# The attention's output projection as fp16 products of high and low halves

## The reference

```
h   = tokeniser(x)                         # three levels, joined, times Wf
n   = layernorm(h)
q, k, v = split(n @ W_qkv);  q = elu(q)+1;  k = elu(k)+1     # 12 heads of 16
kv  = sum over tokens of k^T v;  z = 1 / (q . sum(k) + eps)
att = (q kv) z                             # "the divided rows", 256 x 192 a picture
h   = h + att @ W_out + b_out              # the projection
h   = h + mixture_of_experts(layernorm(h)) # 16 experts, 4 for each token
```

## Time and profile before

| | |
|---|---|
| runs | 592.57, 580.58, 574.64 us; median 580.58 us |
| the profiled execution | 569.85 us, of which the span from the first to the last instruction is 568.0 us |
| PE busy | 422.3 us (74%) |
| DVE busy | 329.8 us (58%) |
| POOL busy | 303.2 us (53%) |
| ACT busy | 249.8 us (44%) |
| mean granted TensorE clock | 0.893 of full speed |
| DMA | 42.64 MB, 75 GB/s on average |

### The profile page before, as it was taken

One profiled execution on the slowest core, in us unless ns is written; L12 is line 12 of the kernel. 1 busy time (PEld: TensorE's weight loads), 2 busy tenths in 40 slices (PEclk: granted clock), 3 DMA queues, 4 the chain that ended last, 5 costly groups with the idle time before them and its releaser, 6 DMA issues.

```text
span 568.0 us, 10275 instructions
## 1 busy us (share of the span) xinstructions
PE 422.3 (74%) x2889; PEld 281.9 (50%) x2889; DVE 329.8 (58%) x836; ACT 249.8 (44%) x570; POOL 303.2 (53%) x362
## 2 busy tenths in 40 slices
PE   0017548488999953399789999999999998899940
PEld 0016115445565642255356666666666666666630
DVE  0567876736465452987346557566666566657530
ACT  1677442244444421111155556555555555556520
POOL 7888810003234422000148888778888887778750
PEclk9999999889789885555589999999999999999995
DMA  8886644600000000001114444444443443443436
GB/s 234 226 232 173 182 129 118 184 2 1 19 25 14 15 15 29 9 28 43 42 47 60 65 67 61 66 67 61 66 66 59 66 68 59 68 66 59 66 37 111
DMA packets 36430, 42.64 MB, mean 75 GB/s; under 512 B 8731, under 2 KB 27693, under 8 KB 36381
## 3 DMA queue, kind: packets, MB, share of 16 engines
q0 software_dynamic: 16976, 18.94, 21.6%
q1 hardware_dynamic: 17694, 22.25, 13.8%
q10 hardware_dynamic: 1710, 0.80, 0.6%
HBM read 27.48 MB, written 14.49 MB: 74 GB/s over the span
## 4 chain that ended last, share of the span: by engine, by line
PE 27%; issue 24%; POOL 18%; DVE 14%; DMA 9%; ACT 4%; SPq 2%; ACTq 0%; DVEq 0%; POOLq 0%
POOL R L358 10%; POOL out L367 3%; DMA R<-t_dram,Li 3%; PE pair L1099 3%; PE pair L1098 2%; DMA R<-in_m 2%; DMA out<-R,Li 2%; POOL acc_odd L367 2%; DVE W1s L396 1%; PE pair L1032 1%; DVE W1s L394 1%; PE pair L934 1%; PE pair L935 1%; PE pair L1033 1%; DVE W2s L398 1%
## 5 line engine op out<-in xcount | busy, mean ns | idle before, releaser
L693 DVE TENSOR_SCALAR R<-pair 128x384 f32<-128x384 f32 x79 | 44.1, 558 | 91.5 <-PE pair L1141 56.4
L358 POOL DMA_INDIRECT R<-t_dram,Li x79 | 81.8, 1035 | 24.3 <-issue 23.1
L367 POOL DMA_INDIRECT out<-R,Li x40 | 64.0, 1600 | 21.3 <-issue 10.6
L1159 PE MATMUL pair<-W2s,R 128*128 x711 | 71.7, 246 | 0.8 <-ACT R L861 0.8
L367 POOL DMA_INDIRECT acc_odd<-R,Li x39 | 63.0, 1616 | 14.3 <-issue 10.4
L849 ACT ACTIVATE R<-pair 128x384 f32<-128x384 f32 x79 | 38.8, 492 | 72.1 <-PE pair L1141 42.2
L297 POOL DMA_INDIRECT R<-in_x,idx_sb x42 | 56.7, 1351 | 13.3 <-issue 12.5
L1159 PEld LDWEIGHTS pair<-W2s,R 128*128 128x128 f16 x711 | 60.5, 98 | 2.6 <-issue 1.0
L1137 PE MATMUL pair<-W1s,R 128*128 x158 | 52.3, 331 | 0.0
L1141 PE MATMUL pair<-W1s,R 67*128 x158 | 52.0, 329 | 0.0
L1139 PE MATMUL pair<-W1s,R 128*128 x158 | 51.7, 327 | 0.0
(11 more groups left out here) (229 smaller groups left out, 826.5 us busy)
## 6 DMA issues: line engine op xcount, KB each, us to landing
h_all<-in_m1a SPq DMA_DIRECT2D x11, 384.0 KB
WQK<-in_m SPq DMA_DIRECT2D x11, 288.0 KB
h_all<-in_m1c SPq DMA_DIRECT2D x11, 192.0 KB
WA<-in_m1a SPq DMA_DIRECT2D x5, 384.0 KB
acc_odd<-lz SPq DMA_DIRECT2D x17, 96.0 KB, 2.0
W1s<-W1s SPq DMA_DIRECT2D x1, 1536.0 KB, 10.4
t_dram<-R SPq DMA_DIRECT2D x8, 192.0 KB, 2.0
out<-h_all SPq DMA_DIRECT2D x8, 192.0 KB, 2.0
```

The costliest lines, as they stand in the source:

```text
L358: po.indirect_dma_start(out=Gr32[:, t % RING, :], out_offset=None, in_=t_dram, in_offset=bass.IndirectOffsetOnAxis(ap=Li[:, t:t + 1], axis ...
L367: po.indirect_dma_start(out=(out, acc_odd)[t % 2], out_offset=bass.IndirectOffsetOnAxis(ap=Li[:, t:t + 1], axis=0), in_=yv[:, t % 4, :], i ...
L693: ve.tensor_scalar(lin[:, p, :], bank[2 + 2 * p][:, 0:HID], (LIMIT + 1) * S1, (1 - LIMIT) * S1, ALU.min, ALU.max).then_inc(s_lin, 1)
L1159: ins = mm(bank[5][:, 0:D], a[:, p, P * m:P * (m + 1)], W2s[:, e, w, D * m:D * (m + 1)], start=k == 0, stop=k == 3 * HC - 1)
```

## The change

The divided rows `att` are split as the other operands are: ACT casts them to fp16 (`high_att`, queued after `copy_tpT` and before `kv_parts`), DVE subtracts for the low half (`low_att`, two instructions, queued between `phi_k` and `phi_q`), and PE transposes the resulting 128 x 384 fp16 rows in three pieces a tile, 6 transposes a picture, where it did 4 in fp32. PE's `att_transposes` waits for `low_att` and no longer for `divide`. `copy_attT` becomes one activation of 128 x 768 fp16 elements. `attT` has one buffer where it had two. `project` is 7 fp16 matmuls a tile: two over a single row (ones times the bias's high and low half) and the five of the pattern above. The result carries the factor 512, which `second_statistics` takes out with a scalar_tensor_tensor in place of the tensor_tensor. Before the loop, ACT and DVE make the halves of the output weights and of the bias, with three more instructions each, in the place of the raw q/k/v weights, which are no longer needed there; SP loads the last 64 rows of the weights twice, and the bias by a DMA of its own that waits for the q/k/v weights to be split. POOL's memset of the ones is gone. The diff, with lines of context left out:

```diff
@@ -78,6 +78,9 @@
         GS = sb("GS", [P, 2, NE])
+        WO16 = WA[:, 0:2 * D].bitcast(F16).rearrange("p (k n) -> p k n", k=4)
+        WOB = WA[0:1, 2 * D:3 * D]
+        WOB16 = WA[0:1, 3 * D:4 * D].bitcast(F16).rearrange("p (k n) -> p k n", k=2)
         GS16 = sb("GS16", [P, 4, NE], F16)
@@ -154,7 +157,8 @@
         att, zz = carve([2, D]), carve([2, 2 * NH])
-        attT = carve([2, 2, 256])
+        attT = carve([3, 256], F16)
+        ar = carve([2, 2 * D], F16)
         tp = carve([2, 2, D])
@@ -188,6 +192,7 @@
+        attb = bank[6][:, 0:384].bitcast(F16)
@@ -208,7 +213,7 @@
         s_phk = sem("s_phi_k"); s_phq = sem("s_phi_q")
-        s_stt = sem("s_state"); s_kvm = sem("s_state_masked"); s_nd = sem("s_num_den"); s_atr = sem("s_att_rows"); s_att_t = sem("s_att_transposed")
+        s_stt = sem("s_state"); s_kvm = sem("s_state_masked"); s_nd = sem("s_num_den"); s_atr = sem("s_att_rows"); s_ath = sem("s_att_high"); s_atl = sem("s_att_low"); s_woh = sem("s_out_weights_high"); s_wol = sem("s_out_weights_low"); s_wob = sem("s_out_bias_loaded"); s_att_t = sem("s_att_transposed")
         s_att = sem("s_attT_copied"); s_o = sem("s_attention_out"); s_h2 = sem("s_h2")
@@ -263,11 +268,14 @@
             sp.dma_start(WO[:, 0, :], wo[0:P, :]).then_inc(s_aw, 16)
-            sp.dma_start(WO[0:D1 + 1, 1, :], wo[P:D + 1, :]).then_inc(s_aw, 16)
+            sp.dma_start(WO[0:D1, 1, :], wo[P:D, :]).then_inc(s_aw, 16)
+            sp.dma_start(WO[D1:P, 1, :], wo[P:D, :]).then_inc(s_aw, 16)
             sp.dma_start(B2[:, :], b2).then_inc(s_aw, 16)
...
+            sp.wait_ge(s_al, 1)
+            sp.dma_start(WOB, wo[D:D + 1, :]).then_inc(s_wob, 16)
             sp.wait_ge(s_z, 1)
@@ -308,8 +316,6 @@
             po.memset(vx[:, :, :, :], 1.0).then_inc(s_ms, 1)
-            po.wait_ge(s_ms, 2)
-            po.memset(attT[D1:D1 + 1, :, 1, :], 1.0).then_inc(s_ms, 1)
@@ -346,7 +352,7 @@
-            po.wait_ge(s_ms, 4)
+            po.wait_ge(s_ms, 3)
@@ -457,7 +463,7 @@
-            ve.wait_ge(s_aw, 16 * 6)
+            ve.wait_ge(s_aw, 16 * 7)
@@ -536,16 +542,22 @@
                 link(ve, ve.reciprocal(z, z))
-                wait(ve, s_att_t, b)
+                wait(ve, s_ath, b)
                 ve.tensor_tensor(att.rearrange("p t (h d) -> p (t h) d", d=HD), nd[:, :, 0:HD],
...
+            def low_att(b):
+                ve.wait_ge(s_ath, b + 1)
+                ve.tensor_tensor(ar[:, :, D:D + D1], att[:, :, P:D], ar[:, :, P:D], ALU.subtract)
+                ve.tensor_tensor(ar[:, :, D + D1:2 * D], att[:, :, 0:P], ar[:, :, 0:P], ALU.subtract).then_inc(s_atl, 1)
+
             def second_statistics(b):
...
                 ve.wait_ge(s_o, b + 1)
-                link(ve, ve.tensor_tensor(h2, h2, bank[6][:, 0:2 * D].rearrange("p (t n) -> p t n", t=2), ALU.add))
+                link(ve, ve.scalar_tensor_tensor(out=h2, in0=bank[6][:, 0:2 * D].rearrange("p (t n) -> p t n", t=2),
+                                                 scalar=1.0 / SQ, in1=h2, op0=ALU.mult, op1=ALU.add))
                 for j in range(2):
@@ -585,6 +597,14 @@
             low_normal(1)
+            ve.wait_ge(s_woh, 1)
+            ve.scalar_tensor_tensor(out=WO16[:, 1, :], in0=WO[:, 0, :], scalar=SQ, in1=WO16[:, 0, :],
+                                    op0=ALU.mult, op1=ALU.subtract)
+            ve.scalar_tensor_tensor(out=WO16[0:D1, 3, :], in0=WO[0:D1, 1, :], scalar=SQ, in1=WO16[0:D1, 2, :],
+                                    op0=ALU.mult, op1=ALU.subtract)
+            ve.scalar_tensor_tensor(out=WOB16[:, 1, :], in0=WOB, scalar=SQ, in1=WOB16[:, 0, :],
+                                    op0=ALU.mult, op1=ALU.subtract).then_inc(s_wol, 1)
+
             phi_k(0)
@@ -600,6 +620,9 @@
                     phi_k(s + 1)
+                if s < NB:
+                    low_att(s)
+                if s + 1 < NB:
                     phi_q(s + 1)
@@ -742,7 +765,7 @@
-            ac.wait_ge(s_aw, 16 * 6)
+            ac.wait_ge(s_aw, 16 * 7)
@@ -752,7 +775,12 @@
                               ACT.Copy).then_inc(s_he, 1)
-            ac.wait_ge(s_ms, 3)
+            ac.wait_ge(s_al, 1)
+            ac.activation(WO16[:, 0, :], WO[:, 0, :], ACT.Copy, scale=SQ)
+            ac.activation(WO16[:, 2, :], WO[:, 1, :], ACT.Copy, scale=SQ)
+            ac.wait_ge(s_wob, 16)
+            ac.activation(WOB16[:, 0, :], WOB, ACT.Copy, scale=SQ).then_inc(s_woh, 1)
+            ac.wait_ge(s_ms, 2)
@@ -785,11 +813,14 @@
             def copy_attT(b):
-                p = b % 2
                 ac.wait_ge(s_att_t, b + 1)
-                wait(ac, s_o, b - 1)
-                ac.activation(attT[:, p, 0, :], bank[6][:, 0:256], ACT.Copy)
-                ac.activation(attT[0:D1, p, 1, :], bank[6][0:D1, 256:512], ACT.Copy).then_inc(s_att, 1)
+                wait(ac, s_o, b)
+                ac.activation(attT.rearrange("p c n -> p (c n)"), attb, ACT.Copy).then_inc(s_att, 1)
+
+            def high_att(b):
+                ac.wait_ge(s_atr, b + 1)
+                wait(ac, s_att_t, b)
+                ac.activation(ar[:, :, 0:D], att, ACT.Copy).then_inc(s_ath, 1)
@@ -818,6 +849,8 @@
                     copy_tpT(s - 2)
+                if s < NB:
+                    high_att(s)
                 if s + 1 < NB:
@@ -835,7 +868,7 @@
-            ac.wait_ge(s_ms, 4)
+            ac.wait_ge(s_ms, 3)
             def copy_tile(t):
@@ -936,10 +969,10 @@
-            pe.wait_ge(s_aw, 16 * 6)
+            pe.wait_ge(s_aw, 16 * 7)
-            pe.wait_ge(s_ms, 3)
+            pe.wait_ge(s_ms, 2)
@@ -1015,22 +1048,28 @@
             def att_transposes(b):
-                p = b % 2
-                pe.wait_ge(s_atr, b + 1)
+                pe.wait_ge(s_atl, b + 1)
                 wait(pe, s_h2, b)
                 for j in range(2):
-                    pe.transpose(bank[6][:, P * j:P * (j + 1)], att[:, j, 0:P], ident)
-                    ins = pe.transpose(bank[6][0:D1, 256 + P * j:256 + P * (j + 1)], att[:, j, P:D], ident)
+                    for c in range(3):
+                        ins = pe.transpose(attb[:, 256 * c + P * j:256 * c + P * (j + 1)],
+                                           ar[:, j, P * c:P * (c + 1)], ident16)
                 ins.then_inc(s_att_t, 1)
...
             def project(b):
-                p = b % 2
+                if b == 0:
+                    pe.wait_ge(s_wol, 1)
                 pe.wait_ge(s_att, b + 1)
...
                     o = bank[6][:, D * j:D * (j + 1)]
-                    mm(o, attT[:, p, 0, t], WO[:, 0, :], start=True, stop=False)
-                    ins = mm(o, attT[0:D1 + 1, p, 1, t], WO[0:D1 + 1, 1, :], start=False, stop=True)
+                    for k in range(2):
+                        mm(o, ones16[0:1, :], WOB16[:, k, :], start=k == 0, stop=False)
+                    mm(o, attT[:, 0, t], WO16[:, 0, :], start=False, stop=False)
+                    mm(o, attT[:, 0, t], WO16[:, 1, :], start=False, stop=False)
+                    mm(o, attT[:, 2, t], WO16[:, 0, :], start=False, stop=False)
+                    mm(o, attT[:, 1, t], WO16[:, 2, :], start=False, stop=False)
+                    ins = mm(o, attT[0:D1, 1, t], WO16[0:D1, 3, :], start=False, stop=True)
                 ins.then_inc(s_o, 1)
...
             def gate(b):
```

## The result

The changed kernel runs in 595.43 us (median; 593.69 to 601.41) against 580.58: slower, ratio 1.047, 95% interval 1.040 to 1.055. The forecast was 585.4 us and no measurable change. The profiled execution took 596.73 us with a span of 594.9.

The account below looks back on a forecast made before the run. Attention passes were taken as bound by PE's chain of waits through `project` and `copy_attT`, or POOL's almost as tight loop. `project` +0.45 and copy +0.17 a pass summed to +4.8 us, on the 580.58 median 585.4; range 575 to 596.

Parts of the forecast that it names:

- The cost of the 14 matmuls: PE's `project`: 14 fp16 matmuls with exposed loads take 1.86 us at full clock, 0.45 more than 1.41.
- the bias pair's load hidden: Between each tile's two single-row bias matmuls in `project`: load taken as hidden; if exposed, 0.2 us more a pass.
- each change of height 0.10: In `project`, a change in the number of stationary rows exposes a load of 0.10 us; six a pass, 0.60.
- the copy: ACT's `copy_attT` as one 128x768 fp16 copy of 0.80 us, adding 0.17 us a pass.
- the cast and subtractions in their holes: ACT's cast (0.52 us) and DVE's two subtractions (0.71 at most) fit in idle holes and cost nothing.
- a forecast 0.62: Added time of each attention pass bound by PE with `project` at full clock: 0.62 us.
- rival 3: In `project`, every weight load stands free: 6.4 us more over eight passes, 592 us; chance 0.03.
- rival 2: In the attention stage TensorE's clock falls more: sum +13.9 us, 594.5 us; chance 0.17.
- its far end: Rival 2 with each of five attention intervals losing 2.93 us: 594.5 us; over 2% slower, 0.06 of its 0.17.
- the clock falls right behind the idle before `project`: Kernel before, interval from 166.06 us: L950 takes 0.85 us there against 0.50 at 156.43; used in rival 1.
- the loss of the worst pass seen, 2.93: Attention interval of 13.97 us against 11.04: 2.93 us lost to half clock, rival 2's loss for each of five.
- the same idle did no harm in two passes: Argument against rival 2: in the passes at 155.02 and 178.62 us the idle before `project` did no harm.

Follow-up runs that it names:

- experiment 1: Kernel before plus only the fp16 high and low halves of the divided rows and PE's wait for them, unused, projection left fp32: 577.14 us.
- experiment 4: Changed kernel plus 12 unread filler matmuls of 128 columns on 128 rows ahead of each `project`: 580.50 us, ratio 1.005.
- experiment 3: Changed kernel with all stationary operands of the projection on 128 rows, the bias's halves in one matmul, 12 matmuls a pass: 574.42 us, ratio 1.002.
- 7: Changed kernel plus 12 filler matmuls of 128 columns ahead of each `project`, their operands cut to 32 rows: 599.94 us, ratio 1.044.
- experiment 2: Kernel before with only the projection as 14 fp16 matmuls a pass; fp32 transposes, no halves or added wait: 602.63 us, ratio 1.053.
- experiment 5: Changed kernel with only the bias matmuls on 128 stationary rows, still two a tile, last product over 64 rows: 592.72 us, no interval.
- 8: Changed kernel without the four single-row bias matmuls of each projection, bias left out of the sum: 571.63 us, ratio 1.008.
- 6: Changed kernel with only each tile's last, 64-row product padded to 128 rows, single-row bias kept: 589.79 us, ratio 1.012.
- experiment 11: Changed kernel with full-row projection, filler, and the experts' bias matmuls padded from 16 to 128 rows: 549.00 us beside 569.24, ratio 0.969.

## Why the prediction was wrong

**Right, and settled by runs.** The cost of the 14 matmuls (1.78 us for a forecast 1.86; the bias pair's load hidden, each change of height 0.10), of the copy (0.79 for 0.80), and the cast and subtractions in their holes, but for 0.15 us a pass (experiment 1). At full clock the change costs 0.52 us a pass for a forecast 0.62 (experiment 4). The rule of the Trainium skill behind rival 3 ("TensorE: Matmul & The Clock Gate", Part 3, What overlaps and what doesn't), that a load is hidden only where the row group differs, does not hold here: L1068 to L1069 stand 0.09 apart with equal heights, and the exposed loads are those where the height differs.

**Wrong: rival 2, its cause, its size and its chance.** The forecast kept the stretches at half clock as they were, and gave 0.17 to more of them. The five middle passes took 61.1 us before and 78.9 after the earlier trace rows, 17.8 more: 2.6 are the 0.52 of each pass, 15.2 the clock. The rest of the 21 is in the first and last intervals, 11.68 for 10.88 and 12.04 for 10.24, and 0.95 before the first projection, where PE waits for the low half (1.03 us idle at 131.35).

That rival 2 priced its far end at 594.5 us, close to the 595.43 measured, is luck: it added 13.9 us to a median that lay 10.7 above the profiled execution, while between the two profiles the stage alone lost 21.

Three things failed in that step. First, the cause: "the clock falls right behind the idle before `project`", said of the earlier trace rows, was read as the pause doing it. The falls do begin behind a pause, but the same pause of 1.51 us does no harm in experiment 3, one of 0.73 us does none in experiment 4 and one of 0.74 does in 7, and in experiment 2 the clock then stays at half for five passes without a pause. What matters is what PE does: the fp32 projection, 4 matmuls over 128 and 65 rows that each take as long as four fp16 ones (0.33 us against 0.083), is replaced by a thinner one in which four of 14 matmuls use one row. With the bias on full rows the falls go back to what they were (experiment 5); 12 filler matmuls hold the clock on 128 rows and not on 32 (4 and 7). That the single rows alone are the cause is not shown: without them three of five passes still fell in the profiled execution (8), and with only the last product padded the executions differ (6). The reading that fits all of them is that the rows in use add up over the matmuls of a pass, and that the single-row ones lower the sum most; how the chip weighs them is not shown.

Second, the size: I took the loss of the worst pass seen, 2.93, as the most that a pass can lose. A pass wholly at half clock costs 17.00 - 11.56 = 5.4; with 16.85 of 17.00 us busy PE then has become the bound of the pass. That could have been worked out from rows: PE was busy for 9.79 us of a pass of 11.04, and most of that doubles.

Third, the chance. The argument against rival 2 was that the same idle did no harm in two passes. But three of five passes lost clock already, so the kernel before was close to the edge, and a change of what PE does there should have been given more than 0.17.

## What to carry to other kernels

Before replacing fp32 matmuls by fp16 ones in a stage that is not dense, look at the granted clock of each pass. If some passes already fall, work out the pass with all of PE's part at half clock and put that in the range. Give a matmul that stands in such a stage all 128 rows, with zero rows if need be: a bias over one row costs an exposed load and the clock, a padded one costs neither. A stage in which PE is busy nearly all the time at a clock of 0.50 (here 36.90 of 39.50 us) is a place to look for thin operands. Padding them gave 12.5 us here, through the exposed loads and the clock together.

## What the runs showed of the hardware

- TensorE at 100% busy for 85 us and at half clock (1.2 GHz) all that time (experiment 2); the same stage with full-row operands at 1.00.
- Twelve fp16 matmuls of 128 columns a pass: on 128 rows clock 1.00 in five passes of five, on 32 rows 0.50 to 0.66 in five of five (experiments 4 and 7).
- Padding with zero rows helped: the added rows hold zeros in the moving operand in experiments 3 and 5, and in both operands in the matmuls of the experts' bias in experiment 11.
- A change of height between two matmuls leaves a load exposed: 0.10 us between fp16 ones at full clock, and 0.30 between the fp32 ones of experiment 11 at half clock (0.94 for 0.64).
- The kernel before is itself near the edge: on one chip its executions ran from 562 us at a mean clock of 0.892 to 583 us at 0.853 (four of 23 at 0.853 or 0.854, where the changed kernel had 0.832 to 0.854), and the kernel of experiment 11 beside it from 548 to 554 us.
